# Cross-attention and LoRA-mixture kernel on one core: division by the softmax sums in PSUM, sums taken ahead of the products with V, their transfers issued by GpSimd, sums of x kept in fp32, weight sums of Q kept in DRAM

## What is computed

```python
def xattn(query, key, value, mask, Wq, Wk, Wv, Wo):      # 32 query heads, 8 key/value heads, size 128
    q = apply_rope((query @ Wq).reshape(b, t, 32, 128))
    k = apply_rope((key @ Wk).reshape(b, t, 8, 128))
    v = (value @ Wv).reshape(b, t, 8, 128)
    logits = 30.0 * tanh(einsum('btkgd,bTkd->bkgtT', q, k) * 0.0884 / 30.0)
    weights = softmax(where(mask, logits, -1e30))
    return einsum('bkgtT,bTkd->btkgd', weights, v).reshape(b, t, 4096) @ Wo

x = x + xattn(layernorm(x), ctx, ctx, mask, Wq, Wk, Wv, Wo)
y = layernorm(x)
base = y @ W_base.T + b_base
rw, sel = top_k(y @ W_router.T, 2); w = onehot(sel) * softmax(rw)
x = x + base + 2 * einsum('ter,te,eor->to', einsum('td,erd->ter', y, A), w, B)
```

## Time and profile before

| | |
|---|---|
| median of 3 runs | 2390.45 us (2382.54 to 2392.41) |
| the profiled execution's own time | 2385.28 us |
| its span | 2383.5 us |
| mean granted TensorE clock | 0.965 |
| TensorE matmuls | 2189.3 us busy (92%), 9409 of them |
| VectorE, ScalarE, GpSimd busy | 75%, 41%, 14% |
| DMA | 474.89 MB, mean 199 GB/s |

### The profile page before, as it was taken

How to read it: one execution, slowest core, us unless ns; L and a number is a source line. 1 busy time by engine, 2 the same in 40 slices (tenths; PEclk the granted TensorE clock), 3 DMA queues, 4 the chain that set the end, 5 groups by cost and what they waited for, 6 DMA issues and landing times.

```text
span 2383.5 us, 26474 instructions
## 1 busy us (share of the span) xinstructions
PE 2189.3 (92%) x9409; PEld 1784.6 (75%) x9409; DVE 1787.5 (75%) x2595; ACT 980.2 (41%) x1524; POOL 344.3 (14%) x217
## 2 busy tenths in 40 slices
PE   8899974999999999969999999997999799879999
PEld 7687863888887888757788777776777688767787
DVE  7777774888879899846677788876898788846533
ACT  3234231222222222245566566655666466413221
POOL 0611700000011100000000001331233122200000
PEclk9899997999999999979999999998999899989999
DMA  9488697333383333468666856675666854674751
GB/s 338 166 306 312 242 350 283 116 119 112 109 331 124 106 111 111 132 196 246 177 177 178 273 173 181 196 246 188 176 202 214 249 151 142 234 262 167 290 212 72
DMA packets 201412, 474.89 MB, mean 199 GB/s; under 512 B 25920, under 2 KB 58816, under 8 KB 195648
## 3 DMA queue, kind: packets, MB, share of 16 engines
q1 hardware_dynamic: 201280, 473.20, 59.9%
HBM read 342.58 MB, written 130.29 MB: 198 GB/s over the span
## 4 chain that ended last, share of the span: by engine, by line
PE 74%; DVE 10%; DMA 10%; issue 2%; ACT 1%; SPq 1%; POOL 1%; DVEq 0%; ACTq 0%; POOLq 0%
PE ps L371 24%; PE ps L372 24%; PE ps L373 24%; DVE Al L327 3%; DMA RB<-rD 3%; DMA rD<-r 2%; DVE AN L327 2%; DMA raw<-gran 2%; DMA XcD<-xst 1%; DVE Rl L327 1%; DVE Y L923 1%; DMA r<-rT 1%; PE ps L859 1%; PE ps L861 1%; DVE Pl L851 1%
## 5 line engine op out<-in xcount | busy, mean ns | idle before, releaser
L371 PE MATMUL ps<-Ah,Rh 128*128 128x512 f32 x1024 | 407.2, 398 | 58.5 <-DVE Al L327 33.3
L372 PE MATMUL ps<-Al,Rh 128*128 128x512 f32 x1024 | 404.7, 395 | 0.0
L373 PE MATMUL ps<-Ah,Rl 128*128 128x512 f32 x1024 | 403.9, 394 | 0.0
L371 PE MATMUL ps<-Xq,qW 128*128 128x512 f32 x896 | 350.8, 392 | 41.6 <-DMA Xq<-XcD 38.3
L372 PE MATMUL ps<-Xq,qW 128*128 128x512 f32 x896 | 349.8, 390 | 0.0
L373 PE MATMUL ps<-Xq,qW 128*128 128x512 f32 x896 | 349.8, 390 | 0.0
L323 ACT ACTIVATE Rh<-raw 128x1024 fp32r<-128x1024 f32 x176 | 186.1, 1058 | 218.9 <-PE ps L373 203.0
L371 PEld LDWEIGHTS ps<-Ah,Rh 128*128 128x128 f32 x1024 | 195.4, 191 | 107.0 <-DVE Al L327 38.8
L327 DVE TENSOR_TENSOR Rl<-raw,Rh 128x1024 fp32r<-128x1024 f32 x161 | 201.3, 1251 | 73.4 <-ACT Rh L323 73.2
L923 DVE TENSOR_TENSOR Y<-ps,Y 128x512 f32<-128x512 f32 x256 | 174.0, 683 | 80.5 <-PE ps L373 79.8
L371 PEld LDWEIGHTS ps<-Xq,qW 128*128 128x128 f32 x896 | 169.0, 189 | 79.2 <-ACT qW L323 32.9
(11 more groups left out here) (212 smaller groups left out, 4297.2 us busy)
## 6 DMA issues: line engine op xcount, KB each, us to landing
raw<-gran SPq DMA_DIRECT2D x177, 512.0 KB, 4.4
qraw<-gran SPq DMA_DIRECT2D x64, 512.0 KB, 4.7
qD<-qt SPq DMA_DIRECT2D x128, 256.0 KB, 2.5
qf<-qD SPq DMA_DIRECT2D x64, 512.0 KB, 7.6
RB<-rD SPq DMA_DIRECT2D x128, 256.0 KB, 5.0
XcD<-xst SPq DMA_DIRECT2D x56, 512.0 KB, 6.7
Xq<-XcD SPq DMA_DIRECT2D x28, 1024.0 KB, 10.0
kraw<-gran SPq DMA_DIRECT2D x32, 512.0 KB, 5.1
```

Of the source, the lines that this page charges most:

```text
L371: put("pe", waits, lambda e: e.matmul(pe_out, lh, rh, start=first, stop=False, skip_group_check=more))
L372: put("pe", [], lambda e: e.matmul(pe_out, lh, rl, start=False, stop=False, skip_group_check=more))
L373: return put("pe", [], lambda e: e.matmul(pe_out, ll, rh, start=False, stop=last, skip_group_check=more), mark)
```

## The change

It has five parts, and the scheduler's table of costs is changed with them.

1. Attention. `att_pv` is cut into `att_den` (the sums, three steps behind the scores), `att_rows` (the RB transfers) and `att_pv` (the product with V, ten steps behind the sums). The multiplication by RB is done in place in the PSUM bank of the product, and the split reads PSUM; the copies `AN` are gone. Seven buffers of `Ph` and `Pl` hold the weights between sums and products (two before). The loads for group gi+2 are cut into those of q and k and that of v.
2. The transfers r<-rT, rD<-r and RB<-rD are issued by GpSimd (`CHAIN = "pool"`), all others still by SP.
3. `x_blocks` stores the seven operands in fp32, without split, half the bytes; `x_load` loads them into the low half of `Xq` and splits them there. `x_stats` of blocks 2 and 3 comes later, and `x_spread` and `x_blocks` are put in the background, a step of TensorE's between diagonal and product.
4. `quad_weights` stores the high and low parts of the four weight sums to DRAM (`QSD`) in the first half of Q, and in the second half loads them in place of making and splitting them.
5. `ln2` takes its first sum by seven additions in place of four reductions, writes x minus mean in place in `Y2` and so needs eight subtractions fewer. The buffer `FY1` of the last stage moves off `Y2`.

```diff
-    COST = {"pe": 227, "act": 630, "dve": 670, "pool": 1480, "sp": 60, "flex": 660}
+    COST = {"pe": 227, "act": 600, "dve": 640, "pool": 1000, "sp": 340, "flex": 640}
-    SEEN, DMA_SEEN, DMA_NS_PER_KB, SLOW, BACKLOG = 90, 2100, 3.6, 2.2, 3
+    SEEN, DMA_SEEN, DMA_NS_PER_KB, SLOW, BACKLOG = 90, 2100, 3.0, 2.2, 2
...
-            elif e == "pool" and not mine and len(ready["dve"]) + len(ready["flex"]) > self.BACKLOG:
-                mine = sorted(ready["flex"], key=lambda r: r[:2])[self.BACKLOG - 1:]
+            elif e == "pool" and not mine and len(ready["dve"]) >= self.BACKLOG:
+                mine = ready["flex"]
...
+            def store(n, k, src, waits, kb, key):
+                d = dma(XcD[cp, n, :, k], src, waits, f"d_xs{key}", kb)
...
-                    d = dma(XcD[cp, n, :, k], f(xst[s][:, :, :]), [h, l], f"d_xs{s}", 512)
...
-                got.append([dma(f(Xq[n][:, 2 * k:2 * k + 2, :, :]), XcD[cp, n, :, 2 * k:2 * k + 2],
-                                x_free[n] + Xc_store[cp, n], f"d_xq{n}{k}", 1024) for k in range(2)])
+                d = [dma(f(Xq[n][:, 2 * k:2 * k + 2, 1, :]), XcD[cp, n, :, 2 * k:2 * k + 2],
+                         x_free[n] + Xc_store[cp, n], f"d_xq{n}{k}", 512) for k in range(2)]
+                got.append([])
+                for k in range(4):
+                    a, b = Xq[n][:, k, 0, :], Xq[n][:, k, 1, :]
+                    h = hi(a, f(b), [d[k // 2]] + x_free[n], "xqh")
+                    got[-1].append([h, lo(b, f(b), a, [h], "xql")])
...
+                if again and key[0] == "S":
+                    yield s, [dma(f(qW[s][:, :, :]), QSD[j, key[1]], free + [qs_store[j, key[1]]], f"d_qw{s}", 512)], []
+                    continue
...
+        def att_den(gi, b):
+            i, z = gi % 2, (4 * gi + b) % NP
+            w = sel[:, 96 - 32 * b:224 - 32 * b]
+            put("pe", p_marks[gi, b] + [m_sel] + (tb_free[0] if b == 0 else []), lambda e: e.matmul(
+                Tb[:, :], w, Ph[z][:, :], start=b == 0, stop=False))
...
+            st = dma(r16[i][:, :], rT[i][0:P:32, :], [r] + r16_free[i], f"d_rt{i}", 8, CHAIN)
+            rt_free[i] = [st]
+            r = put("dve", [st], lambda e: e.reciprocal(r16[i][:, :], r16[i][:, :]), cn("dve_o"), 200)
+            st = dma(rD[i].rearrange("r (i t) -> (r i) t", t=16), r16[i][:, :], [r] + rd_free[i], f"d_rs{i}", 8, CHAIN)
...
+            a = tt("dve", o, o, RB[:, b, :], ALU.mult, [m, rb_marks[gi][b]], "an")
+            rb_free[b] = [a]
+            h = hi(Ah[:, rows, dst], v4(o), [a] + a_war[i], "ah")
+            l = lo(Al[:, rows, dst], v4(o), Ah[:, rows, dst], [h] + a_war[i], "al", "dve")
+            ob_free[n] = [h, l]
...
+        for gi in range(len(groups)):
+            s0, u = 8 * gi - 21, 2
+            if gi == 0:
+                s0, u = -16, 1
+            plan.setdefault(s0 + (11 if u == 2 else 7), []).append((att_rows, gi, 0))
+            for b in range(4):
+                plan.setdefault(s0 + u * b, []).append((att_s, gi, b))
+                plan.setdefault(s0 + u * b + (3 if u == 2 else 2), []).append((att_den, gi, b))
+                plan.setdefault(s0 + u * b + (13 if u == 2 else 9), []).append((att_pv, gi, b))
```

More of the change, by code:

```diff
@@ L207, in program @@
         mv = sb("mv", [P, C, 4, 2], F32)
-        ln_at = top[0]
+        r16 = [sb(f"r16{i}", [P, 16], F32) for i in range(2)]
         L1 = sb("L1", [P, T], F32)
@@ L719, in quad_weights @@
                 read["raw" if key[0] == "raw" else key].extend([h, l])
-                slots.append((s, [h, l]))
-                yield slots[-1]
+                kept = []
+                if key[0] == "S":
+                    kept = [dma(QSD[j, key[1]], f(qW[s][:, :, :]), [h, l], f"d_qk{s}", 512)]
+                    qs_store[j, key[1]] = kept[0]
+                yield s, [h, l], kept
             qraw_free[n % 2] = read["raw"]
-            for i in range(4):
-                sf[i] = read["S", i]
+            if not again:
+                for i in range(4):
+                    sf[i] = read["S", i]
         def q_quad(cp, j, n, x_marks):
@@ L735, in product @@
             def product(i, dst, first, waits):
-                s, wm = next(weights)
+                s, wm, kept = next(weights)
                 for k in range(4):
@@ L795, in program @@
                   "v": [list(x_free[3]), list(x_free[3])]}
-        qhl_free = [list(x_free[4]) for _ in range(4)]
+        qhl_free = [list(x_free[4]) for _ in range(2)]
         a_war = {0: x_free[5] + x_free[6], 1: x_free[5] + x_free[6]}
```

327 lines of the change are left out of this document (154 added, 173 removed).

## The result

The changed kernel takes 2212.93 us (median of 4 runs, 2210.62 to 2214.08), the kernel before 2386.49 us beside it: a ratio of 0.927, with an interval of 0.9244 to 0.9296. Forecast were 2267 us and 2215 to 2330. The profiled execution took 2210.62 us, its span is 2208.8, its granted clock 0.991.

What follows compares the result with a forecast made beforehand. TensorE bounds the kernel, 253 of 2383.5 us lost to waits and lower clock; 60 + 38 + 10 - 2 + 6 + 8 = 120 off 2385.3 gives 2265, stated as 2267 us, range 2215 to 2330.

Steps and rivals of the forecast that it cites:

- Attention, 60 forecast: Attention: of 99 us lost, long waits, restarts and shorter waits give back 60; bounds 20 and 85.
- Three waits that SP made: Attention: three TensorE waits of about 12 us, 36.6 in all, go when the transfers leave SP's list.
- I take half, 17 us: Attention: half of the shorter waits for Al (20.9) and for Pl (13.5) goes, 17 us.
- restarts 7.5: Attention: TensorE's slow start after each of three long waits costs 2.5 us, so 7.5 are gained.
- Work in PSUM, and VectorE beside GpSimd: Attention: VectorE's work in PSUM is steadier, as GpSimd slows only two-SBUF-operand operations; multiplication at 0.69 us, within the 17 us.
- The chain: Attention, last sums to first product with V: copy, three transfer hops and reciprocal take 12.5 us within 13.4; wrong above 15.
- The late chain: Rival, chance 0.20: hops 2 us longer make attention's chain 18.5, 5 late per group; attention gains 15, kernel 2310.
- K and V to Q with the first spread: Stages ahead of Q: 38 us gained from K and V to Q, 10 at the first spread.
- Half turn: Half turn of Q: 28 added splits on VectorE lose 2 us; bounds +3 and -8.
- Q to attention: Border from Q to attention: waits for weights of V shrink, gain 6 us; bounds -5 and 15.
- last stage: Last stage: the wait of 5.4 us for FY and its restart of 2.5 go, gain 8; bounds 0 and 15.
- Slower (0.05): Rival, chance 0.05: attention's hops of 7 us each make the chain 22.7, kernel 2408; decides from about 6.6 a hop.

Runs made afterwards that it cites:

- e1: The changed kernel with the chain's four kinds of transfers issued by SyncE again: 2209.01 us, ratio 0.9263, not told apart from the changed kernel.
- e4: The kernel before with the chain's transfers issued by GpSimd alone: 2411.68 us, ratio 1.0111, slower than before.
- e9: The kernel before with scores, sums and products four jobs earlier, 180 matmuls of lead in place of 116: 2318.15 us, ratio 0.9728.
- e16: The kernel before with 180 matmuls of lead, sums three jobs after the scores, and the new table of costs with its rule: 2249.73 us, ratio 0.9426.
- e6: The changed kernel with a shorter window between sums and products, normalising in SBUF through AN again: 2249.70 us, no difference from the short window alone.
- e7: The changed kernel with VectorE's product written over RB in SBUF and split from there: 2213.16 us, no difference from the changed kernel.
- e3: The kernel before with only the new table of costs and the new rule for GpSimd: 2318.02 us, ratio 0.9711.
- e2: The changed kernel with the old table of costs and the old rule for GpSimd: 2234.73 us, 22 slower than the changed kernel.
- e8: The changed kernel with x's path (statistics, spread, block sums and their loads) as before: 2262.97 us, ratio 0.949.
- e11: The changed kernel without the stores and reloads of Q's weight sums, which are computed and split again: 2213.07 us.
- e17: The changed kernel with FY's first load held until two base jobs have run and the last layernorm 2 later: 2203.05 us, ratio 0.9236.
- e10: The kernel before with 180 matmuls of lead and the new table of costs with its rule: 2290.73 us, ratio 0.9612.
- e12: The changed kernel with the second group's q, k, v held for Q's last product and FY's first load for the router's job: 2211.64 us.

## Why the prediction was wrong

The direction and the order of size held (0.91 for faster); the time fell 2 us below the range, since the gains sum to 174.7 us of span where 120 were forecast. That the range comes so near is an error's doing: its lower end is said to be 50 below the forecast, but the four terms named for it (20, 7, 3 and 7) sum to 37, which is 2230.

- **Attention, 60 forecast, 93.1 measured.** This step failed, in size and in mechanism. "Three waits that SP made" was read off one of them, and misread: of the 14.5 us from rD<-r to RB in the earlier trace rows the landing of rD<-r took 11.7, the longest of the earlier trace rows, and SP's list 2.8. e1 and e4 refute it as the cause. In its place: the lead between a group's last sums and its first `o_job`, 116 matmuls against 194. The prediction has the 59 and the 34 matmuls and the 114 of before in view, asks only whether the chain fits into the 59, and never sets the whole against the whole. Lead gives 71.4 (e9), the third step with the table 7.2 more (e16), and the last 14.5 were not separated.
- **"I take half, 17 us" and "restarts 7.5".** Nearly all short waits went, and with them the slow steps behind them: in the kernel before, TensorE's steps of over 1 us from one matmul to the next lose 67.1 us in attention against 0.2264 a step, and those of 0.25 to 1 us 27.2; in e9 19.1 and 7.8; in the changed kernel 2.4 and 0.6. The upper bound of 85 left the small steps in, and they belong to the waits.
- **Work in PSUM, and VectorE beside GpSimd.** The multiplication is at 0.69 us as said, and worth nothing (e6, e7, e9).
- **The chain.** Forecast 12.5 us, "wrong above 15". The 2.9 taken for r<-rT is not its own: the earlier trace rows has the landings of rD<-r alone, and r<-rT's, by its semaphore, took 5.0 in the median before, and 2.3 in the changed kernel. From the copy of the sums to the first multiplication 14.7 us pass in most groups, with RB there; where layernorm 2 runs, up to 21.8. Tiles r and RB of the changed kernel, from issue to landing, and then the same of e1, where tile r has rD<-r alone:

```profile
DMA to landing us min/median/max: 1.7/2.2/7.7
...
DMA to landing us min/median/max: 3.4/8.6/11.7
```

```profile
DMA to landing us min/median/max: 1.4/2.0/6.7
...
DMA to landing us min/median/max: 3.1/5.7/11.5
```

So GpSimd's RB did land later, 8.6 us against the 5 that were allowed; yet e1's chain takes 14.7 us in the median too. The late chain (chance 0.20) came true in part: four groups took over 18 us, and VectorE waited 13.8 us for RB in all (0.4 a group, as said), TensorE 0.2 for Al. Its price was wrong, for it charged to TensorE what the lead takes up. GpSimd's list in the worst group (start, us, idle before it and its releaser):

```profile
1485.99 0.72 POOL L319 DMA_DIRECT2D r<-rT  x1 [18.84 <-ACT rT L888]
1492.01 0.55 POOL L319 DMA_DIRECT2D rD<-r  x1 [5.31 <-DVE r L892]
1499.98 2.16 POOL L319 DMA_DIRECT2D RB<-rD  x4 [7.41 <-DMA rD<-r]
```

- **The table of costs** had no term. Alone it is worth 66 us on the kernel before (e3), and 22 in the changed kernel (e2). A schedule's numbers are an edit like any other.
- **K and V to Q with the first spread, 48 forecast, 57.5 measured**, and the wait of 5.6 us behind the first product, counted there, went as well. x's path gives 32 ahead of Q (e8), the table 15 to 26. TensorE's waits there (vst 4.0, qW 1.5) are below the 15 named.
- **Half turn, -2 forecast.** Q gained 11.7, of which 5.6 are the wait just named. Costing QSD at nothing was right (e11), on a condition that was not written down: in e8, with Xq's loads of twice the size, the reloads cost 12.7.
- **Q to attention, 6 forecast, 1.7 measured; last stage, 8 and 10.7.** The first is a wait that moved: from weights of V to kT and Vl. In the last stage the table alone gives 16 (e3), and old costs in the changed kernel make that stage 6 faster (e2); with loads taken away from ahead of the router's weights it is 7.5 faster (e17).
- **Slower (0.05)** needed three hops of over 6.6 us (6.8 by its own terms). RB's was 8.6, those of r<-rT and rD<-r 2.3 and 1.8, and GpSimd waited 75.7 us for rD in 31 groups, 2.4 each. The Trainium skill (DMA: Bandwidth & Descriptors, Latency and other measured facts) has the first byte of a GpSimd transfer later than SP's: the right sign for RB (8.6 us against e1's 5.7), not for rD<-r (1.8 against 2.0). Of the Trainium skill's rule that VectorE locks GpSimd out of the descriptors' ports (SBUF — State Buffer, SBUF: two separate sides) no run here shows the long case: GpSimd's issues take 546 to 840 ns, and the late chain that the estimate by it led to did not cost what it said.

## What to carry to other kernels

When work is moved, count the bottleneck's instructions from the first producer to the last consumer, before and after, and set that against the whole side chain in its worst group, with each small transfer's landing read from its own row; which engine issues it is second. Do not divide a stage's loss into waits and small change: on TensorE the slow steps go when the waits go. Take the scheduler's costs and each distance apart in runs of their own, since one may hurt without the other (e10 against e16), and where a load is held back, look at which needed transfer it meets next, or the wait may only move (e12; in e17, which held it longer and moved one more load, it did not).
